# Spreading two pairs of norm rows by TensorE, an own order for the first four tiles, and identity transposes in TensorE's waits

## The reference

```python
xn = layernorm(x, ln1_w, ln1_b)          # over 256 columns
yn = layernorm(y, ln2_w, ln2_b)          # over 192 columns, y is the context
q = (xn @ Wq).reshape(B, N1, H, hd).transpose(0, 2, 1, 3)      # 16 heads of 16
kv = (yn @ Wkv).reshape(B, y.shape[1], 2, H, hd)
attn = softmax(einsum('bhqd,bhkd->bhqk', q, k) * scale)
x = x + (einsum('bhqk,bhkd->bqhd', attn, v) @ Wproj + bproj)
...                                       # then layernorm, W1, gelu, W2, and the second attention layer
```

## Time and the profile before

| what | value |
|---|---|
| median of 3 runs | 395.61 us (394.93 to 397.18) |
| the profiled execution, its own time | 397.7 us |
| its span in the trace | 395.9 us |
| instructions | 11443 |
| busy share of the span: PE, PEld, DVE, ACT, POOL | 90%, 81%, 75%, 60%, 50% |
| DMA traffic | 12.84 MB, mean 32 GB/s |

### The profile page before, as it was taken

The page is one execution under the profiler, slowest core; times in us unless marked ns, Lnnn a source line. Parts: engine busy times, 40 slices in busy tenths (PEclk is TensorE's granted clock), DMA queues, the critical chain, the costliest instruction groups (busy, mean ns, idle before and its releaser), DMA issues.

```text
span 395.9 us, 11443 instructions
## 1 busy us (share of the span) xinstructions
PE 358.2 (90%) x4448; PEld 321.9 (81%) x4448; DVE 295.1 (75%) x655; ACT 238.0 (60%) x461; POOL 197.1 (50%) x177
## 2 busy tenths in 40 slices
PE   7596999999999998989999999979798998998974
PEld 7576788888888876788999999979687887887853
DVE  3777888898899965149655576656899989999752
ACT  1343666667766574826344675171887877877762
POOL 2453354454576620103212331338889899899820
PEclk9886999999999999999999999999999999999999
DMA  6941210000000000000000000000000100110001
GB/s 157 281 132 56 85 51 25 27 26 25 25 3 2 22 2 2 2 2 2 0 0 0 0 1 1 12 10 12 12 21 12 49 26 23 46 36 13 26 30 41
DMA packets 15000, 12.84 MB, mean 32 GB/s; under 512 B 3056, under 2 KB 14320, under 8 KB 14960
## 3 DMA queue, kind: packets, MB, share of 16 engines
q1 hardware_dynamic: 13888, 11.17, 9.5%
q10 hardware_dynamic: 1072, 1.11, 1.0%
HBM read 10.18 MB, written 2.10 MB: 31 GB/s over the span
## 4 chain that ended last, share of the span: by engine, by line
PE 60%; issue 21%; DVE 8%; ACT 5%; POOL 4%; DMA 2%; ACTq 0%; POOLq 0%; DVEq 0%
PE bank_qk L662 9%; PE banks_s L710 7%; PE bank_qk L687 4%; PE bank_y L797 4%; PE bank_qk L691 4%; PE bank_t L763 4%; PE bank_y L791 3%; PE bank_o L701 3%; PE banks_s L963 3%; PE bank_t L662 3%; DMA ln_rows<-in_L_xattn_ln_b 2%; POOL x_all L360 2%; PE bank_y L983 2%; PE bank_o L952 2%; PE banks_s L745 1%
## 5 line engine op out<-in xcount | busy, mean ns | idle before, releaser
L398 POOL TENSOR_TENSOR norm_inv<-norm_sq_min,minus_half 128x32 f32<-128x32 f32 x16 | 87.4, 5466 | 1.8 <-DVE norm_sq_min L1297 1.8
L541 ACT ACTIVATE W_s<-banks_s,b_cols 128x256 f32<-128x256 f32 x60 | 25.0, 469 | 41.3 <-PE banks_s L846 41.3
L336 POOL TENSOR_TENSOR masked<-qkT_r,halves_t 128x512 fp32r<-128x512 f32 x32 | 32.8, 1047 | 30.1 <-DVE qkT_r L1124 30.1
L1134 DVE TENSOR_REDUCE row_max<-banks_s 128x8 f32<-128x1024 f32 x32 | 37.7, 1218 | 9.7 <-PE banks_s L710 9.7
L465 ACT ACTIVATE PT<-banks_s 128x1024 f32<-128x1024 f32 x32 | 31.0, 1022 | 21.8 <-PE banks_s L745 19.7
L353 POOL TENSOR_TENSOR b_var_eps<-b_mean_var,eps_t 128x2 f32<-128x2 f32 x8 | 1.6, 197 | 69.0 <-DVE b_mean_var L1068 69.0
L846 PE MATMUL banks_s<-lnT_hi,W_hi 128*128 128x256 f32 x120 | 34.2, 285 | 0.0
L846 PE MATMUL banks_s<-lnT_lo,W_hi 128*128 128x256 f32 x120 | 33.9, 283 | 0.0
L846 PE MATMUL banks_s<-lnT_hi,W_lo 128*128 128x256 f32 x120 | 33.9, 283 | 0.0
L710 PE MATMUL banks_s<-masked,qkT_r 32*128 32x256 f32 x768 | 32.2, 298 | 1.6 <-DVE row_max L1134 1.4
L710 PEld LDWEIGHTS banks_s<-masked,qkT_r 32*128 32x128 f32 x768 | 25.6, 188 | 9.9 <-issue 8.2
(11 more groups left out here) (158 smaller groups left out, 1096.1 us busy)
## 6 DMA issues: line engine op xcount, KB each, us to landing
ctx_in<-in_ctx SPq DMA_DIRECT2D x32, 96.0 KB, 2.1
x_all<-in_x SPq DMA_DIRECT2D x16, 128.0 KB, 2.1
W_s<-in_L_xattn_W SPq DMA_DIRECT2D x2, 1024.0 KB, 6.7
out<-Wq_s SPq DMA_DIRECT2D x16, 128.0 KB, 1.7
Wq_s<-in_L_xattn_Wq ACTq DMA_DIRECT2D x1, 256.0 KB, 6.9
Wkv_s<-in_L_xattn_Wkv ACTq DMA_DIRECT2D x1, 256.0 KB, 7.3
Wproj_s<-in_L_xattn_Wproj SPq DMA_DIRECT2D x1, 256.0 KB, 4.3
wout_s<-in_L_xattn_wout SPq DMA_DIRECT2D x1, 256.0 KB, 2.9
```

The source lines that it names most:

```text
L336: nc.gpsimd.tensor_tensor(masked[:, r, 1, :, half, :], qkT_r[:, r, 1, :, :].bitcast(fp32), ones, ALU.mult)\
L398: nc.gpsimd.tensor_tensor(norm_inv[:, j, :], norm_sq_min[:, j, :], minus_half[:, :], ALU.pow)\
L541: last = nc.scalar.activation(hT[:, m, :], (bank or bank_s[u])[:, 256 * k:256 * k + 256], ACT.Gelu, bias=b1_cols[:, m:m + 1])
L1134: v.tensor_reduce(row_max[:, 8 * h:8 * h + 8], banks_s[:, 2 * h:2 * h + 2, :].rearrange("p n (r k) -> p (n r) k", k=TOK), AX.X, ALU.max).t ...
```

## The change

Four parts, all within the first four tiles of stage A:

1. The four row loads of ScalarE's queue now bring each row once, into one partition (1 KB, 1 KB, 768 bytes, 768 bytes; into `PT`, which is unused so far). TensorE multiplies a row of ones with them (two fp32 matmuls, 512 and 384 columns wide, one partition deep) into `bank_qk` and `bank_o`, and ScalarE copies the two banks to `ln1_rows` and `ln2_rows`. `normalise(0)` waits for these copies.
2. The loads of `Wq` and `Wkv` move from ScalarE's queue to SP's, between tile 0 and tile 1 of x and context.
3. All five engines' programs for steps 1 to 4 are replaced by orders of their own. ScalarE copies the transposed inputs of a tile before it masks the keys of the tile before; it also widens `picks_wide`, which was VectorE's. `maxima_a(0)` goes through `bank_y`. From step 5 on, nothing is changed.
4. The 48 turns of the identity matrix become 14 before the row matmuls and 26 behind them, and 31 more (8, 5, 10, 8) stand at four places of TensorE's order for tiles 0 to 3.

```diff
-WARM = 48
+WARM_EARLY, WARM_LATE = 14, 26
...
+        row_1, row_2 = PT[0:1, 0, :], PT[0:1, 1, 0:2 * C2]
+        one_row = vals[0:1, :, :, :].rearrange("p j h w -> p (j h w)")[:, 0:128]
...
             load_in(0, 0, in_loaded)
+            sp.dma_start(Wq_s[:, :, :], Wq.rearrange("(t p) n -> p t n", p=128)).then_inc(w_q_loaded, LOADED)
+            sp.dma_start(Wkv_s[:, 0, :], Wkv[0:128, :]).then_inc(w_att_loaded, LOADED)
+            sp.dma_start(Wkv_s[0:C2B, 1, :], Wkv[128:C2, :]).then_inc(w_att_loaded, LOADED)
             load_in(1, 1, in_loaded)
...
             residual_bias(0)
+            inverse_std(2)
+            masked_lo(0)
             residual_bias(1)
-            masked_lo(0)
+            residual_bias(2)
+            inverse_std(3)
+            masked_lo(1)
+            residual_bias(3)
+            masked_lo(2)
+            inverse_std(4)
+            residual_bias(4)
+            masked_lo(3)
...
-            for s in range(2, NB + 1):
+            for s in range(5, NB + 1):
                 step_a(s)
...
-                act.dma_start(ln1_rows[:, n, :], v.unsqueeze(0).broadcast_to([128, C1])).then_inc(ln_rows_loaded, LOADED)
+                act.dma_start(row_1[:, C1 * n:C1 * n + C1], v.unsqueeze(0)).then_inc(ln_rows_loaded, LOADED)
...
-                act.dma_start(ln2_rows[:, n, :], v.unsqueeze(0).broadcast_to([128, C2])).then_inc(ln_rows_loaded, LOADED)
-            act.dma_start(Wq_s[:, :, :], Wq.rearrange("(t p) n -> p t n", p=128)).then_inc(w_att_loaded, LOADED)
-            act.dma_start(Wkv_s[:, 0, :], Wkv[0:128, :]).then_inc(w_att_loaded, LOADED)
-            act.dma_start(Wkv_s[0:C2B, 1, :], Wkv[128:C2, :]).then_inc(w_att_loaded, LOADED)
+                act.dma_start(row_2[:, C2 * n:C2 * n + C2], v.unsqueeze(0)).then_inc(ln_rows_loaded, LOADED)
...
+            act.wait_ge(rows_spread, 1)
+            nc.scalar.activation(ln1_rows[:, :, :], bank_qk[:, :].rearrange("p (n c) -> p n c", n=2), ACT.Copy).then_inc(rows_ready, 1)
+            nc.scalar.activation(ln2_rows[:, :, :], bank_o[:, 0:2 * C2].rearrange("p (n c) -> p n c", n=2), ACT.Copy).then_inc(rows_ready, 1)
             act.wait_ge(ones_ready, 1)
             inputs_T(0)
             act.wait_ge(halves_loaded, 2 * LOADED)
-            for s in range(1, NB):
+            nc.scalar.activation(picks_wide[:, :, :], each(picks_t[:, :], GH, TOK), ACT.Copy).then_inc(picks_ready, 1)
+            queries_keys_hi(0)
+            inputs_T(1)
+            masked_hi(0)
+            values_a(0)
+            queries_keys_hi(1)
+            inputs_T(2)
+            masked_hi(1)
+            values_a(1)
+            queries_keys_hi(2)
+            maxima_T(0, bank_y)
+            inputs_T(3)
+            masked_hi(2)
+            exps_a(0)
+            queries_keys_hi(3)
+            masked_hi(3)
+            out_T(0)
+            values_a(2)
+            maxima_T(1)
+            inputs_T(4)
+            for s in range(5, NB):
                 step_a(s)
...
+            def busy(count):
+
+                for n in range(count):
+                    nc.tensor.transpose(bank_y[:, 0:128], ident[:, :], ident[:, :])
+
             pe.wait_ge(ident_ready, 2)
-            for n in range(WARM):
+            for n in range(WARM_EARLY):
+                nc.tensor.transpose(bank_s[n % 4][:, 0:128], ident[:, :], ident[:, :])
+            pe.wait_ge(ln_rows_loaded, 4 * LOADED)
+            pe.wait_ge(ones_ready, 1)
+            mm(bank_qk[:, :], one_row, row_1, start=True, stop=True)
+            mm(bank_o[:, 0:2 * C2], one_row, row_2, start=True, stop=True).then_inc(rows_spread, 1)
+            for n in range(WARM_LATE):
                 nc.tensor.transpose(bank_s[n % 4][:, 0:128], ident[:, :], ident[:, :])
             inputs_a(0)
-            pe.wait_ge(w_att_loaded, 3 * LOADED)
+            pe.wait_ge(bank_zeroed, 1)
+            busy(8)
+            pe.wait_ge(w_q_loaded, LOADED)
+            pe.wait_ge(w_att_loaded, 2 * LOADED)
             pe.wait_ge(w_padded, 1)
-            step_a(1)
+            queries_keys_a(0)
+            inputs_a(1)
+            values_a(0)
+            busy(5)
+            queries_keys_a(1)
+            busy(10)
+            scores_a(0)
+            inputs_a(2)
+            values_a(1)
+            queries_keys_a(2)
+            scores_a(1)
             pe.wait_ge(picks_ready, 1)
-            step_a(2)
-            step_a(3)
-            pe.wait_ge(bank_zeroed, 1)
-            step_a(4)
+            busy(8)
+            maxima_a(0, bank_y)
+            inputs_a(3)
+            values_a(2)
+            shifted_a(0)
+            queries_keys_a(3)
+            scores_a(2)
+            weighted_a(0)
+            maxima_a(1)
+            inputs_a(4)
+            back_a(0)
+            shifted_a(1)
             pe.wait_ge(w_out_loaded, 2 * LOADED)
             for s in range(5, NB):
                 step_a(s)
...
-            dve.wait_ge(ln_rows_loaded, 4 * LOADED)
+            dve.wait_ge(rows_ready, 2)
             normalise(0)
             statistics(1)
             normalise(1)
-            dve.wait_ge(halves_loaded, 2 * LOADED)
-            v.tensor_copy(picks_wide[:, :, :], each(picks_t[:, :], GH, TOK)).then_inc(picks_ready, 1)
             dve.wait_ge(a_padded, 2)
+            statistics(2)
             queries_keys_lo(0)
-            for s in range(2, 5):
-                step_a(s)
+            normalise(2)
+            statistics(3)
+            queries_keys_lo(1)
+            maxima(0)
+            normalise(3)
+            queries_keys_lo(2)
+            maxima(1)
+            statistics(4)
+            normalise(4)
+            queries_keys_lo(3)
+            maxima(2)
             w1_split(0)
             w1_split(1)
```

More of the change, by code:

```diff
@@ L188, in build @@
         a_padded, w_padded, c_padded = sem("a_padded"), sem("w_padded"), sem("c_padded")
-        ln_rows_loaded, picks_ready = sem("ln_rows"), sem("picks_ready")
+        ln_rows_loaded, picks_ready, w_q_loaded = sem("ln_rows"), sem("picks_ready"), sem("w_q")
+        rows_spread, rows_ready = sem("rows_spread"), sem("rows_ready")
         w1_hi_done, w1_lo_done, w2_hi_done, w2_lo_done = (sem(k) for k in ("w1_hi_done", "w1_lo_done", "w2_hi_done", "w2_lo_done"))
@@ L729, in maxima_a @@
                         pe.wait_ge(a_qk_lo, upto(t + 3))
+                    elif bank is bank_y:
+                        pe.wait_ge(bank_zeroed, 1)
                     else:
@@ L819, in step_a @@
                 shifted_a(s - 3)
+            def busy(count):
+                for n in range(count):
+                    nc.tensor.transpose(bank_y[:, 0:128], ident[:, :], ident[:, :])
             pe.wait_ge(ident_ready, 2)
-            for n in range(WARM):
+            for n in range(WARM_EARLY):
[5 more added lines that the diff above has]
+            for n in range(WARM_LATE):
                 nc.tensor.transpose(bank_s[n % 4][:, 0:128], ident[:, :], ident[:, :])
             inputs_a(0)
-            pe.wait_ge(w_att_loaded, 3 * LOADED)
+            pe.wait_ge(bank_zeroed, 1)
+            busy(8)
+            pe.wait_ge(w_q_loaded, LOADED)
+            pe.wait_ge(w_att_loaded, 2 * LOADED)
             pe.wait_ge(w_padded, 1)
-            step_a(1)
-            pe.wait_ge(picks_ready, 1)
-            step_a(2)
-            step_a(3)
-            pe.wait_ge(bank_zeroed, 1)
-            step_a(4)
+            queries_keys_a(0)
[9 more added lines that the diff above has]
+            scores_a(1)
+            pe.wait_ge(picks_ready, 1)
+            busy(8)
[10 more added lines that the diff above has]
+            shifted_a(1)
             pe.wait_ge(w_out_loaded, 2 * LOADED)
```

## The result

The changed kernel took 385.74 us in the median of four executions (385.62 to 388.68), the kernel before 396.39 (394.93 to 397.45); the ratio is 0.9747, with a 95% interval of 0.9696 to 0.9798. So it became faster, by 10.65 us where 9.4 were forecast. A second comparison on another chip, with more executions, is less kind: 390.4 (385.98 to 391.66) against 395.9, ratio 0.9848, interval 0.9802 to 0.9895. The first comparison has two further executions, 391.67 and 385.64, that are not in its median; the first of them lies over 1.5% above the fastest and was set aside as slow. Of all twelve executions five lie at 385.6 to 386.0, three at 388.7 to 389.7, four at 391.1 to 391.7; their mean is 388.5. Much of what follows is about what separates these groups.

The account below looks back on a forecast made before the run. TensorE was taken to set the time from step 5 on. Step 5 9.6 us earlier, less 0.2, gave 9.4 (rows 1.2, half clock some 3, order the rest): 395.6 - 9.4 = 386.2 us, forecast span 384.5 to 388, range 384 to 391.

Parts of the forecast that it names:

- given back: Rival: the gain at step 5 turns into TensorE waits on VectorE or loads until 125; 394 to 397 us, chance 0.06.
- The row matmuls: Two fp32 matmuls spreading the rows at the start: 2.6 us taken, from 1.5 with early clock rise to 2.8 at half clock.
- Copies and landing: Start of stage A: rows land at 4.6 us, ScalarE's two copies take 1.1, so rows are ready at 8.3.
- The late turns: 26 turns behind the row matmuls: 2.8 us, covered by the first norm, price 0; upper bound 2.7 on the path.
- the clock rival: First four tiles: the clock is not kept, one-partition matmuls perhaps counting little; gain 4.5 to 7.5 us, chance 0.18.
- The walk through tiles 0 to 3: New order at full clock: queries of tile 0 at 11.5, `shifted_a(0)` ends 28.85, step 5 at 36.2 instead of 45.82.
- The weights: `Wq` and `Wkv` on SP's queue land by 6 to 8, needed at 11.4: the move is covered by 3 us.
- The slower rival: SP's queue: a late `bproj` row holds GpSimd's `inverse_std(2)`, the norm of 2 and the scores; 398 us if at 26, chance 0.04.
- Of this 1.2 is the rows: Share of the 9.4 us gain given to spreading the rows at the start of stage A: 1.2 us.
- some 3 the half clock on the path, the rest the order: Split of the 9.4 us beside the rows: some 3 us half clock, the rest inputs ahead of masks and norms in waits.
- The sum: Step 5 comes 9.6 us earlier, less 0.2 for VectorE's W1 splits: 9.4 us gained, 386.2 us forecast.
- more gained: Case for the first tiles: turns end early, rows ready at 7.0; 384 us and below, chance 0.04.

Follow-up runs that it names:

- deep rows: Changed kernel with the rows loaded into partition 96, those ahead zeroed by VectorE, and row matmuls 97 partitions deep; 387.83 us, ratio 0.9799.
- wide rows: Changed kernel with each row loaded 128 times again, no row matmuls or copies, 48 turns in one piece at the start; 387.67 us, ratio 0.9805.
- order alone: Wide rows without the 31 turns, leaving the own order of tiles 0 to 3 and the weights on SP's queue; 389.12 us, ratio 0.9854.
- turns alone: Kernel before, old order and rows, with 31 turns (8, 15, 8) in TensorE's waits of steps 1 to 3; 392.90 us, ratio 0.9919.
- weights held back: Wide rows with 14 and 22 turns, and SP waiting for the rows before it loads the weights; 389.71 us, ratio 0.9841.
- deep rows with 22 late turns: Deep rows with 22 late turns instead of 26 and 18 more turns at the end of stage B; 387.69 us, ratio 0.9813.

## Why the prediction was right, and where it was not

**What bounds the kernel.** The prediction was right here. From step 5 on TensorE alone sets the time, steps are 8.33 apart, and what was gained ahead of it was kept. The rival "given back" did not occur.

**The row matmuls.** Mis-sized. "I take 2.6, since the earlier turns reached full rate only near 6"; they took 3.28, above my upper 2.8. Copies and landing were right (1.0 us; TensorE started on the rows at 4.7), so the norm began at 9.12 and not at 8.3.

**The late turns.** This is the step that failed: "The 26 later turns cost 2.8 at 0.11 [...] I take 0". They took 4.41 and 5.47 us in the two traces, of which 1.6 and 2.65 lay behind the end of the norm. I had the bound (2.7 on the path) and the rival that a one-partition matmul "may count as little", but gave it 0.18 together with the rest of the clock rival. The deep rows show what matters: with the same columns at the same place, 97 partitions deep, the rate rose near 7 and near 6 in two traces. With one partition it rose between 11 and 13.4 in all five traces that had 14 turns ahead of the row matmuls. Where full-depth turns stood there alone (the kernel before, wide rows, order alone, turns alone, weights held back) it rose between 5 and 7.3. The rival's other half, half clock in queries and keys, did not occur in these traces: the clock column is 1.00 from 12.7 to 36.2, also behind the wait of 1.34 us ahead of `shifted_a(0)`.

The Trainium skill, TensorE: Matmul & The Clock Gate, "What's actually happening", says that activity releases the throttle. The traces with full-depth turns or deep rows agree. The five with one-partition matmuls differ: TensorE was busy without a pause from 4.79 on, and the full rate still came only at 11 to 13.4.

**The walk through tiles 0 to 3.** Right in its intervals. From the queries of tile 0 to step 5 I had 24.7 us, measured were 24.43; queries of 0 to those of 1 were 3.9 and 3.70; `shifted_a(0)` ended 17.35 behind the queries of 0 in the walk, and 17.2 in the trace (30.90). Only its start was late, 13.69 instead of 11.5. Of the 0.5 and 1.1 us that I charged to the turns of five and ten, 0.74 showed on TensorE's way to the first scores and nothing at step 5.

**The weights.** Right that the move is covered: no matmul of the changed kernel waits for a load up to 38. The slower rival did not occur. That these loads are not far from the path is shown by holding them back.

**How the gain is made up.** My attribution was wrong. "Of this 1.2 is the rows": the spread rows lose 1.3 to 2.4 us against wide rows with the same order and turns (step 5 at 36.78 against 38.12 and 39.20), and 0.4 in the old order; they gain 1.0 to 1.5 only when the full rate comes early (35.81 and 35.26 with deep rows). And "some 3 the half clock on the path, the rest the order" was the other way round, if the estimate above holds: some 7 us clock and some 2 us order, of the 8.9 that the own order brings, with the weights' move in it. The turns bring 3.4 in the old order and 0.2 in step 5 beside the new one.

**The sum.** 386.2 was forecast and 385.74 measured, but not by the way of the sum; that the two lie within half a microsecond is luck. Step 5 came 1.9 us later than forecast in the traced execution, and the traced pair made up 1.3 of it by the half clock at 265 to 269 in the kernel before. The three other executions of the first comparison were 3 us shorter than the traced one (spans 383.8 to 384.0 against 386.9). A rise of the rate ahead of the row matmuls would shorten them by 1.6 and take 1.6 off the late turns, together 3.2. That it can rise as early as 5.0 is in the trace of the turns alone. The deep rows with 22 late turns, whose rate rises early, have in fact a span of 383.9 with step 5 at 35.26. That these executions were such is argued and not shown, as none was traced. With twelve executions in view the gain is nearer 7.5 us (396 to 388.5) than 9.4. One slip in the prediction's own chances: the three cases outside its range (more gained, given back, slower) add up to 0.14, not 0.12.

## What to carry to other kernels

An order of its own for the first steps of a pipeline, which puts what the next engine needs ahead of what only the same tile needs, was here worth more than any other part, and by estimate mostly because TensorE then waits so little that its clock does not fall. Turns of the identity in the waits of the old order gave back less than half as much. Walk such an order once with measured durations. Before a load is replaced by matmuls, look at the rate at which TensorE runs at that moment: here the one-partition matmuls at the start ran at half rate, and the full rate came only 3 to 5 us behind them; with 97 partitions the same step gained. And compare a stretch that ends ahead of the noise (here the start of step 5), since two medians of four executions differed by more than the part under test.

## What was not expected of the hardware

- TensorE's clock column read 1.00 while a turn of the identity took 0.21 us instead of 0.11, until 5 to 13.4 us after the start, by the trace. The durations show the rate there, the column does not.
- Matmuls one partition deep, 3.28 us of them in one piece, did not bring the full rate in five traces (rise at 11 to 13.4 us); 97 partitions deep it came in both traces (near 6 and 7 us).
- The same program with the same start to 0.01 us up to 8.00 reached full rate near 11.1 in one execution and near 13.1 in another, and the three groups of its times span 6 us.
- Behind the same wait of 2.30 us at the passage to stage C the clock fell to half in six traces (one of them that of the kernel before) and stayed full in six others (one of them the first of the changed kernel). It cost 1.5 us (12.81 against 11.32). Eighteen turns in that wait left the lower mean clock in nine of thirteen executions.
